# The code rows of the second alignment: difference by GpSimd in bf16 in place of two fp32 products on TensorE

## What is computed

```python
def _align_one(small, large):            # small: latents (64), large: context (1601)
    D = _pairwise_euclidean(small, large)
    R = _dtw_cost(D)                     # r = d_ij + min(up, left, diag)
    i_idx, j_idx, valid = _backtrack(R, T_small, T_large)
    contrib = small[i_idx] * valid[:, None]
    return jnp.zeros((T_large, d)).at[j_idx].add(contrib)
...
x = x + _L0_xattn_ref(ctx_1024, _layernorm(x))        # the alignment, contexts summed along the path
x = x + _L0_attn_ref(_layernorm(x), Wr, Wk, Wv, Ww, Wo)
x = x + _L0_ffn_ref(_layernorm(x), gate_w, w1, w2, w3, sw1, sw2, sw3)
```

## Time and profile before

| | |
|---|---|
| median of three runs | 1104.49 us (1102.95 to 1105.37) |
| profiled execution, its own time | 1107.17 us |
| its span, first to last instruction | 1105.9 us |
| mean granted TensorE clock | 0.955 |
| forward sweep of group 1 on VectorE | 333.4 to 493 us, its last code row 504.7 us |
| backward sweep of group 1 | 504.7 to 592.7 us, path terms 596.2 us |

### The profile page before, as it was taken

How to read it: one execution, slowest core, us unless ns; L and a number is a source line. 1 busy time by engine, 2 the same in 40 slices (tenths; PEclk the granted TensorE clock), 3 DMA queues, 4 the chain that set the end, 5 groups by cost and what they waited for, 6 DMA issues and landing times.

```text
span 1105.9 us, 15528 instructions
## 1 busy us (share of the span) xinstructions
PE 995.2 (90%) x4892; PEld 593.8 (54%) x4892; DVE 636.3 (58%) x2310; ACT 498.4 (45%) x851; POOL 115.8 (10%) x150
## 2 busy tenths in 40 slices
PE   5999788898935999989996998897999999999998
PEld 2334233343313555645674656475767676676776
DVE  7988799989996783887995123455111111111116
ACT  6989577767832545334322552431222222222222
POOL 2000000000000000000000000002334344342110
PEclk9999899999976999989998998988999999999999
DMA  9999885656859896520600982961212122223015
GB/s 353 320 352 347 286 279 156 209 157 217 263 134 348 262 302 199 161 75 1 198 1 8 352 263 78 335 231 57 71 58 89 51 86 62 81 63 112 24 51 198
DMA packets 123823, 190.48 MB, mean 172 GB/s; under 512 B 8800, under 2 KB 92928, under 8 KB 123744
## 3 DMA queue, kind: packets, MB, share of 16 engines
q1 hardware_dynamic: 117712, 170.72, 47.6%
q0 software_dynamic: 5888, 18.36, 5.4%
q10 hardware_dynamic: 144, 0.41, 0.2%
HBM read 165.43 MB, written 24.03 MB: 171 GB/s over the span
## 4 chain that ended last, share of the span: by engine, by line
PE 70%; DVE 14%; ACT 5%; DMA 4%; issue 4%; SPq 3%; POOL 0%; ACTq 0%; DVEq 0%; POOLq 0%
PE bank L1954 14%; PE bank L1801 8%; PE bank L1985 8%; PE bank L1946 5%; PE bank L1822 5%; PE bank L1712 4%; PE bank L1728 4%; PE bank L1977 4%; PE bank L1729 4%; PE bank L1965 3%; DVE beyond L950 2%; ACT sq L1416 2%; PE bank L1949 2%; DVE passed L956 2%; PE bank L1706 2%
## 5 line engine op out<-in xcount | busy, mean ns | idle before, releaser
L1142 DVE TENSOR_TENSOR hid<-bank,act_s 128x352 f32<-128x352 f32 x104 | 54.1, 523 | 216.7 <-PE bank L1954 178.8
L1954 PE MATMUL bank<-w_up,srcT 128*128 x512 | 162.8, 460 | 0.8 <-ACT srcT L1567 0.8
L1575 ACT ACTIVATE act_s<-bank 128x352 f32<-128x352 f32 x104 | 48.0, 464 | 203.3 <-PE bank L1954 113.4
L1954 PEld LDWEIGHTS bank<-w_up,srcT 128*128 128x128 f32 x512 | 96.0, 189 | 47.9 <-issue 4.1
L1712 PE MATMUL bank<-sq,ones 128*64 128x402 f32 (+1 forms) x512 | 99.5, 509 | 18.2 <-ACT sq L1416 18.2
L1801 PE MATMUL bank<-rows_c,on_path 128*64 128x256 f32 (+1 forms) x832 | 101.5, 397 | 5.1 <-DMA rows_c<-ctx_nat_dram 4.2
L1706 PE MATMUL bank<-ctxT,latT 128*64 128x402 f32 (+1 forms) x512 | 101.4, 518 | 3.6 <-DMA ctxT<-ctx_tr_dram 2.7
L1416 ACT ACTIVATE sq<-ctxT 128x1608 f32<-128x1608 f32 x64 | 97.6, 1527 | 9.5 <-DMA ctxT<-ctx_tr_dram 9.5
L1728 PE MATMUL bank<-table,ident 128*128 128x402 f32 x144 | 66.7, 546 | 35.5 <-DVE stays L893 29.7
L933 DVE TENSOR_TENSOR_SCAN table<-col_min,table 128x201 f32<-128x201 f32 x140 | 88.5, 632 | 14.7 <-issue 12.5
L1985 PE MATMUL bank<-w_dn,hidT 128*128 (+1 forms) x384 | 93.6, 380 | 0.4 <-DVE y_sb L1156 0.4
(11 more groups left out here) (304 smaller groups left out, 1576.4 us busy)
## 6 DMA issues: line engine op xcount, KB each, us to landing
rows_c<-ctx_nat_dram SPq DMA_DIRECT2D x32, 896.0 KB
ctxT<-ctx_tr_dram SPq DMA_DIRECT2D x32, 804.0 KB, 7.4
ctxT<-ctx_tr_dram SPq DMA_DIRECT2D x32, 797.0 KB, 8.2
rows_c<-ctx_nat_dram SPq DMA_DIRECT2D x32, 640.0 KB
spaced<-dist SPq DMA_DIRECT2D x128, 101.0 KB, 4.6
w_up<-w_t_dram SPq DMA_DIRECT2D x16, 704.0 KB, 12.8
table<-spaced SPq DMA_DIRECT2D x7, 808.0 KB, 12.3
table<-spaced SPq DMA_DIRECT2D x28, 202.0 KB, 3.7
```

Of the source, the lines that this page charges most:

```text
L1954: last = e.matmul(psum[2 * i + m][:, 0:HH], srcT[t % 2][:, k, :], w_up[:, bass.ds(ex, 1), m, k, columns], start=(k == 0), stop=(k == KC - 1))
```

## The change

The second group's table-minus-minima is formed by GpSimd, 18 instructions of up to 804 columns that read two fp32 operands and write bf16 into `code[1]`. TensorE then needs only two bf16 products for each half: the difference by a bf16 identity (`same`, a new tile, made by one VectorE copy in the set-up) and the tie-break. The first group stays as it was. TensorE takes the halves of a group two and three steps after it ends, where it took them one and two after; ScalarE's halves come one step later as well. VectorE's wait for a `col_min` buffer is now on GpSimd (`differed`). The three tables of pieces have other numbers; the pieces themselves are the same.

```diff
+            def code_difference(q):
+                k0, n, i = q * CB, code_width(q), minima_slot(1, q)
+                e.wait_ge(step_done, scan_value(1, k0 + n - 1))
+                e.wait_ge(stayed, CODES + q + 1)
+                if q:
+                    e.wait_ge(differed, q)
+                e.tensor_tensor(code[1][:, k0:k0 + n, 0:L], table[1][:, k0 + 1:k0 + n + 1, 0:L], col_min[i][:, 0:n, :],
+                                ALU.subtract).then_inc(differed, 1)
+
+            for q in range(CODES):
+                code_difference(q)
...
+                e.tensor_copy(same[:, :], ident[:, :]).then_inc(set_up, 1)
...
                     if at == 0 and q >= places_:
-                        e.wait_ge(gapped, half_count(g, q - places_, 1))
+                        if g:
+                            e.wait_ge(differed, q - places_ + 1)
+                        else:
+                            e.wait_ge(gapped, half_count(g, q - places_, 1))
...
                 e.wait_ge(stayed, g * CODES + q + 1)
+                if g:
+                    e.wait_ge(differed, q + 1)
+                    e.matmul(gap, same[:, :], code[1][:, k0:k0 + n, 0:L], start=True, stop=False)
+                    e.matmul(gap, tie[:, :], stays[i][:, 2 * h:2 * h + n, 0:L], start=False, stop=True).then_inc(gapped, 1)
+                    return
...
+    if g:
+        if n == STEPS:
+            return [(CODES - 2, 1), (CODES - 1, 0), (CODES - 1, 1)]
+        return [(q, at - 2)] if q >= 0 and at in (2, 3) else []
...
 BESIDE_SECOND = [int(n) for n in (
-    "000000111011101110211001101120111011011211111111212001122101010111011111"
+    "000010000021001111020110400022000101202020112201132011022002032010000200"
...
 SHARED_BESIDE = [int(n) for n in (
-    "0000000000000101001011010000000000010000")]
+    "0000000000001101001011010020101001100000")]
```

More of the change, by code:

```diff
@@ L227, in half_steps, with code_halves, bar_halves @@
     return range(q * CB + 2 * h, min(STEPS, q * CB + 2 * h + 2))
-def code_halves(n):
+def code_halves(g, n):
     q, at = n // CB - 1, n % CB
+    if g:
+        if n == STEPS:
+            return [(CODES - 2, 1), (CODES - 1, 0), (CODES - 1, 1)]
+        return [(q, at - 2)] if q >= 0 and at in (2, 3) else []
     if n == STEPS:
         return [(CODES - 1, 0), (CODES - 1, 1)]
-    return [(q, at - 1)] if q >= 0 and at in (1, 2) and n < STEPS else []
-def bar_halves(n):
+    return [(q, at - 1)] if q >= 0 and at in (1, 2) else []
+def bar_halves(g, n):
     q, at = n // CB - 1, n % CB
+    if g:
+        if n == STEPS:
+            return [(CODES - 2, 0), (CODES - 2, 1), (CODES - 1, 0), (CODES - 1, 1)]
+        if at == 0:
+            return [(q - 1, 1)] if q >= 1 else []
+        return [(q, 0)] if q >= 0 and at == 3 else []
     if n == STEPS:
         return [(CODES - 2, 1), (CODES - 1, 0), (CODES - 1, 1)]
-    return [(q, at - 2)] if q >= 0 and at in (2, 3) and n < STEPS else []
+    return [(q, at - 2)] if q >= 0 and at in (2, 3) else []
 def half_count(g, q, h):
@@ L280 @@
 BESIDE_SECOND = [int(n) for n in (
-    "000000111011101110211001101120111011011211111111212001122101010111011111"
-    "02001100201101022011000100100010001000100111000000100100100010001000001")]
+    "000010000021001111020110400022000101202020112201132011022002032010000200"
+    "21010002010101110111000100310120000000000111002000000010013010000100000")]
 VECTOR_BESIDE_SECOND = [int(n) for n in (
-    "000000011101110111011101021111110110112111101111112011111102011211121011"
-    "01110020110110101011000011100100010000100010010001000011000100011000000")]
+    "000000001031002010001220022002000011104100110300111121022102010041300202"
+    "10020002011011002001000111000101000100001001000011000010001000011000101")]
 SHARED_BESIDE = [int(n) for n in (
-    "0000000000000101001011010000000000010000")]
+    "0000000000001101001011010020101001100000")]
 def behind_second(n):
@@ L477, in build @@
         assert cursor[0] <= align_end
+        at(table_at[0] + PATH + HALF_TILES - P * 2)
+        same = place("same", [P], BF16)
+        assert cursor[0] <= table_at[1]
         at(table_at[0] + PATH)
@@ L552, in build @@
             sem(n) for n in ("step_done", "stayed", "gapped", "barred", "edged", "coded", "back_done", "termed", "spread"))
+        differed = sem("differed")
         numbered, shaped, terms_kept, terms_in = sem("numbered"), sem("shaped"), sem("terms_kept"), sem("terms_in")
@@ L580, in build @@
         BUILT = 17
-        SET_UP = 11
+        SET_UP = 12
         PADDED = 16 * GROUPS
@@ L1469, in align @@
                 for n in range(CODE_SLOTS):
-                    for q, h in bar_halves(n):
+                    for q, h in bar_halves(g, n):
                         code_bar(g, q, h)
@@ L1733, in align @@
                 for n in range(CODE_SLOTS):
-                    for q, h in code_halves(n):
+                    for q, h in code_halves(g, n):
                         code_gap(g, q, h)
```

## The result

The changed kernel takes 1098.68 us (median of 20 runs, 1094.31 to 1109.37), the kernel before 1104.4 us beside it (20 runs): a ratio of 0.9945, with a 95% interval of 0.9924 to 0.9967, about 6.1 us less. The forecast was 1096 in 1084 to 1111. The profiled execution of after takes 1099.38 us, against 1107.17.

What follows compares the result with a forecast made beforehand. TensorE bounds the forward sweep now, VectorE's floor afterwards: 359 + 108.3 + 15.6 + 14 = 496.9 against 504.7 us, 7.8 less, and 1.0 less backward. In all -8.8 us, rounded to 1096, range 1084 to 1111.

Steps and rivals of the forecast that it cites:

- VectorE's holds: Forward sweep: 12 exposed GpSimd differences hold VectorE 1.3 us each, about 70% of 1.8, 15.6 us in all.
- Held for the whole instruction: Rival, chance 0.29: each of 12 differences holds VectorE the full 1.8 us, 21.6 us; time 1100.
- No hold at all: Rival, chance 0.16: GpSimd's reads don't hold VectorE; waits 18.5 us, last code row at 485.8, time 1085.
- GpSimd's instruction: Second group's difference on GpSimd: 1.8 us for 804 columns, between bounds 0.73 and 2.86 us.
- Slower: Rival, chance 0.20: GpSimd pays both inputs in full, 2.86 us; break-even hold 2.2 us; time 1111.
- The floor: VectorE's forward sweep: busy time and issue gaps without waits, 108.3 us from the sum of pair 0.
- TensorE sheds 40 us: Forward stretch: 34 halves each save 1.18 us as two fp32 products become one bf16, about 40 us.
- The first sum: Sum of pair 0, for which VectorE waits before the forward sweep: taken at 359, before at 359.49.
- I take 14 us with a slower sweep: VectorE's remaining forward waits: 15.5 us of two-engine chains, 3 more for step 52, partly hidden, taken as 14.
- I leave its 92.1 us, less 1.0: Backward sweep: stays at 92.1 us, less 1.0 because the last `xr` addition moves ahead of the path terms.
- The context rows don't stop it: Forward sweep's row transfers: 9.4 us a pair, seven pairs end near 425 us, ahead of the step needing the last.
- It gives nothing: Rival, chance 0.05: row transfers or their issue order keep 14 us a pair; only 1.0 us is left.

Runs made afterwards that it cites:

- write_only: Changed kernel with GpSimd's difference replaced by two index-pattern writes of the same shape that read nothing; ratio 0.9894 to the kernel before.
- Double: Changed kernel with every GpSimd difference from code group 1 on done twice, one behind the other; ratio 1.0127 to the kernel before.
- gpsimd_only: Changed kernel's GpSimd difference and two bf16 products, but all three tables of pieces as before the change; ratio 1.0113 to the kernel before.
- late_ws: Changed kernel with SyncE's loads of the shared expert's weights issued after the context rows of pairs 4 to 7; ratio 0.9948 to the kernel before.
- paused: As columns, plus a small GpSimd instruction ahead of each group's third and fourth column, late shared-expert loads and a changed VectorE table; 1094.84 us, ratio 0.9912.
- columns: Changed kernel with GpSimd's difference cut into single columns, released over the next four steps; ratio 0.9971 to the kernel before.

## Why the prediction came out as it did

The total was nearly right, and so was the mechanism on VectorE. But two errors of about 5 us cancelled, 5.9 us too little in the forward sweep and 4.5 too much in the backward one. That the total came so close is luck to this extent.

- **VectorE's holds** were the term on which most hung: 12 x 1.3 = 15.6 us, measured 16.0 in 12 holds. The exempt ones were right too (those ahead of the first sum, behind steps 52 and 60, the last). The reason given for 70% was wrong: shuffles and readers of PSUM don't shorten a hold. The scan that already runs isn't interrupted, and has used 0.5 us of GpSimd's time before the minimum comes. *Held for the whole instruction* put 1.8 us on each hold; the instruction lasts 1.95, but a hold only 1.3. *No hold at all* is excluded by the minima of 1.65 us, and write_only, where these vanish with the reads, prices them: its forward stretch fell by 6 us of the 16.
- **GpSimd's instruction** took 1.95 us, and 1.32 for the last 603 columns, against 1.8 taken between 0.73 and 2.86. The Trainium skill (GPSIMD Engine Reference, Elementwise — side-by-side cycle accounting) gives an estimate of 1.77 us in proportion to its 2048 elements; the measured value is above it, and decides. *Slower* needed holds of 2.2 us: not reached. Double shows that its mechanism works: 1.3% slower than before once there are twice as many.
- **The floor** was predicted at 108.3 us and is 108.6.
- **TensorE sheds 40 us**: the half's two products start 0.17 us apart, as priced, but busy time fell by 29.3 us. The granted clock is 0.84 in the stretch where it was 0.96, and other products take longer: the 28 at 413.10 need 5.47 us, those of the earlier trace rows 3.24. TensorE isn't the bound, but VectorE waits for chains through it, and what slower products cost there isn't shown.
- **The first sum** came 2.1 us earlier after the first scan, forecast 0.5. The first 28 row products start at 352.55 us. Less the 3.5 us by which this execution is late, that is 349.0, as forecast. They take 5.04 us where 6 were taken, the 24 behind them 2.81 as forecast, and the rest is the rounding up to 359. Just ahead of them TensorE waits for GpSimd's second difference (3.85 us), and neither of the two groups waits for rows. Kernels with the changed order there range from 22.8 to 26.4 us, and gpsimd_only, with the old order, has 23.6, so the distance isn't clearly the change's to set.
- **"I take 14 us with a slower sweep"** is the step that failed in the forward sweep: the waits are 20.8. The 15.5 us of chains were to grow by 3 and then shrink to 14 as a slower sweep hides them. Only `kv` shrank, from 8.8 to 4.4. `decay` rose from 3.0 to 5.9: the 11.1 us of the earlier trace rows are gone, as said, but 4.6 us for the same `decay` stand in their place. That "a lighter TensorE" takes them away whole was the wrong cause, since gpsimd_only keeps 9.7 with a light TensorE. The additions gathered in step 52 cost 7.4 us with their rms (2.9 + 0.3 + 4.2), where the same rows had 3.2 before: 4.2 more, and 3 had been added. `lg` rose from 0.2 to 2.2, which no term had. Against the sum: waits +6.8, holds +0.4, floor +0.3, first sum -1.6: the last code row 5.9 us later than forecast, seen from the first scan.
- **"I leave its 92.1 us, less 1.0"** failed the other way: 86.6. The 1.0 us was right as far as it goes, for the last `xr` addition now stands ahead of the path terms and the first of their two products releases the weights:

```profile
592.54 1.29 DVE L1054 TENSOR_TENSOR path_terms<-feature,own 128x128 f16<-128x128 f16 x2
592.88 0.93 PE L1813 MATMUL bank<-path_terms,row_terms 128*128 128x128 f16 x7 [5.33 <-DVE path_terms L1054]
```

  But the new numbers of the tables' second half were read for that alone. Four other waits went too, and two recurrence instructions moved forward.
- **"The context rows don't stop it"** was wrong as to the trace, with 7.3 us of waiting TensorE, and right as to the end, as late_ws shows. *It gives nothing* by the transfers is excluded with it.

## What to carry to other kernels

When work goes to GpSimd, price what its reads do to the VectorE instructions with two SBUF inputs beside it (and its writes, to a tensor_scalar or a cast): as long as GpSimd's instruction lasts, less what runs already. Cut short enough for one VectorE instruction to cover it, and released once that one runs, it took 8 us less of VectorE's time (paused against after); that the kernel is faster by it than after isn't shown. A schedule table that comes with a change is a change of its own, over its whole length: price it entry by entry, and don't call a wait a backlog before a kernel with the load taken away has lost it.

## What the hardware showed

- A VectorE tensor_scalar with a single SBUF tensor and two per-partition operands (`hn`, fp32, 128x256) was held as well, 1.78 us for 0.39. I had priced only instructions with two SBUF inputs. Unlike the minima, it is held by GpSimd's writes too (1.02 us in write_only), and so was a cast (0.48 us for 0.17). The Trainium skill (the same section of SBUF — State Buffer) has tensor_scalar and cast among those that can meet GpSimd, by way of modes that take two ports at once and when their operands fit. The trace agrees as to the holds; it doesn't show the mode.
- The size of what is held doesn't matter: a tensor_tensor of 4 columns took 1.57 us for 0.13.
- The loser of a meeting isn't always VectorE: where the scan started first, one GpSimd column took 0.75 to 0.81 us, and 0.61 or 0.62 where the scan was the one held. In columns, two that met the 1.22 us scan of `kv` took 1.47 us.
- TensorE's granted clock was lower in a stretch where it idles for 26% (0.84) than where it idles for 5% (0.96); behind the 7.3 us of idling, 28 row products took 5.47 us at a granted 0.58, and the 24 behind them 2.81, in proportion the full pace again.
